# Causal scores of two heads in shared rows: an even head that needs 64 fewer keys per tile

## The reference

```python
q = (hidden_states @ Wq.T).reshape(bsz, q_len, N_HEADS, HEAD_DIM).transpose(0, 2, 1, 3)
q = q * cos + _rotate_half(q) * sin
k = jnp.repeat(k, GROUPS, axis=1)      # GROUPS = 4 query heads for each key head
v = jnp.repeat(v, GROUPS, axis=1)
scores = jnp.einsum('bhqd,bhkd->bhqk', q, k) * scale
scores = jnp.where(causal[None, None], scores, -1e9)
attn = jax.nn.softmax(scores, axis=-1)
out = jnp.einsum('bhqk,bhkd->bhqd', attn, v)
return out.transpose(0, 2, 1, 3).reshape(bsz, q_len, N_HEADS * HEAD_DIM) @ Wo.T
```

## Time and profile before

| what | value |
|---|---|
| median of 3 runs | 1459.31 us (1459.26 to 1460.89) |
| span of the profiled execution (first to last instruction) | 1457.5 us |
| granted clock of TensorE, mean | 1.000 |
| PE busy | 98% |
| DVE, POOL, ACT busy | 79%, 70%, 69% |
| DMA | 322.03 MB, 221 GB/s over the span |

### The profile page before, as it was taken

The page is one execution under the profiler, slowest core; times in us unless marked ns, Lnnn a source line. Parts: engine busy times, 40 slices in busy tenths (PEclk is TensorE's granted clock), DMA queues, the critical chain, the costliest instruction groups (busy, mean ns, idle before and its releaser), DMA issues.

```text
span 1457.5 us, 24651 instructions
## 1 busy us (share of the span) xinstructions
PE 1430.5 (98%) x7150; PEld 1208.2 (83%) x7150; DVE 1153.7 (79%) x3544; ACT 1006.8 (69%) x2389; POOL 1023.1 (70%) x805
## 2 busy tenths in 40 slices
PE   7989999999999999999999999999999999999998
PEld 7877888888888888888888888888888888888886
DVE  5697777777777777787777777777779998998876
ACT  5667666776776676767676677677677676776674
POOL 3767766876776677667676767677588888887662
PEclk9999999999999999999999999999999999999999
DMA  9478765875677667676677667758788899889872
GB/s 305 157 210 250 225 193 182 239 235 152 204 227 218 187 212 228 190 206 211 184 216 233 220 180 208 202 178 257 228 239 259 269 295 262 284 256 270 270 229 67
DMA packets 215157, 322.03 MB, mean 221 GB/s; under 512 B 42512, under 2 KB 132464, under 8 KB 215024
## 3 DMA queue, kind: packets, MB, share of 16 engines
q1 hardware_dynamic: 214736, 320.39, 73.7%
q10 hardware_dynamic: 288, 0.07, 0.0%
HBM read 179.43 MB, written 140.95 MB: 220 GB/s over the span
## 4 chain that ended last, share of the span: by engine, by line
PE 85%; POOL 4%; DVE 4%; DMA 2%; issue 2%; ACT 2%; SPq 0%; DVEq 0%; ACTq 0%
PE bank_s L634 22%; PE bank_o L794 21%; PE bank_pv L744 14%; PE bank_s L700 13%; PE bank_s L666 5%; PE bank_s L651 5%; POOL PT_lo L1836 2%; PE bank_s L696 1%; PE bank_s L607 1%; PE bank_s L850 1%; DVE y L1540 1%; DMA PT_raw<-blocks 1%; POOL qT_lo L1829 1%; DMA wc_scratch<-wc_out 1%; DVE blocks L1488 0%
## 5 line engine op out<-in xcount | busy, mean ns | idle before, releaser
L1836 POOL TENSOR_TENSOR PT_lo<-PT_raw,PT_hi 128x640 fp32r<-128x640 f32 x246 | 382.2, 1576 | 30.4 <-ACT PT_hi L1126 30.4
L1112 ACT ACTIVATE probs<-probs,row_inv 128x512 f32<-128x512 f32 (+3 forms) x512 | 257.8, 553 | 192.1 <-DVE row_inv L1471 192.1
L1824 POOL TENSOR_TENSOR rot_c<-rot_c,rot_s 128x512 f32<-128x512 f32 x128 | 167.7, 1310 | 257.7 <-DVE rot_s L1428 257.7
L1105 ACT ACTIVATE probs<-probs,row_min 128x384 f32<-128x384 f32 (+3 forms) x512 | 281.6, 552 | 49.2 <-DVE row_min L1464 49.2
L1488 DVE STREAM_TRANSPOSE blocks<-probs 128x384 f32<-128x384 f32 x508 | 213.7, 446 | 21.2 <-ACT probs L1112 13.0
L700 PE MATMUL bank_s<-kT_both,qT_hi 128*128 128x512 f32 (+2 forms) x768 | 215.2, 341 | 3.0 <-issue 1.3
L1464 DVE CUSTOM_DVE_ANT_0 probs<-bank_s,mask 128x512 f32<-128x512 f32 (+2 forms) x384 | 205.5, 552 | 0.8 <-issue 0.3
L1829 POOL TENSOR_TENSOR qT_lo<-rot_c,qT_hi 128x512 fp32r<-128x512 f32 x128 | 167.0, 1304 | 51.0 <-ACT qT_hi L1087 50.2
L634 PE MATMUL bank_s<-hT_lo,wq_hi 128*128 128x512 f32 x484 | 194.8, 403 | 2.2 <-DVE row_min L1464 1.4
L794 PE MATMUL bank_o<-wo_lo,OT_hi 128*128 128x512 f32 x496 | 195.1, 393 | 0.5 <-DVE rot_s L1428 0.5
L794 PE MATMUL bank_o<-wo_hi,OT_hi 128*128 128x512 f32 x496 | 193.4, 390 | 0.0
(11 more groups left out here) (315 smaller groups left out, 3255.0 us busy)
## 6 DMA issues: line engine op xcount, KB each, us to landing
blocks<-blocks SPq DMA_DIRECT2D x127, 640.0 KB, 3.5
PT_raw<-blocks SPq DMA_DIRECT2D x500, 160.0 KB, 3.9
stage<-in_wq SPq DMA_DIRECT2D x32, 256.0 KB, 5.1
vblocks<-kv_raw SPq DMA_DIRECT2D x32, 256.0 KB, 5.4
kv_raw<-vblocks SPq DMA_DIRECT2D x128, 64.0 KB, 2.3
stage<-in_wo SPq DMA_DIRECT2D x32, 256.0 KB, 5.1
split_wq<-wq_hi SPq DMA_DIRECT2D x32, 256.0 KB, 5.4
split_wq<-wq_lo SPq DMA_DIRECT2D x32, 256.0 KB, 5.7
```

The costliest lines, as they stand in the source:

```text
L1105: ins = act.activation(row(t, qt), row(t, qt), ACT.Exp, bias=row_min[m][:, qt:qt + 1], scale=-1.0, accum_out=row_sum[m][:, qt:qt + 1])
L1112: ins = act.activation(row(t, qt), row(t, qt), ACT.Copy, scale=row_inv[t % 2][:, qt:qt + 1])
L1824: pool.tensor_tensor(rot_c[:], rot_c[:], rot_s[:], ALU.add).then_inc(pool_a, 1)
L1836: pool.tensor_tensor(lo[:, at], raw_of(t)[:, at], hi[:, at].bitcast(F32), ALU.subtract).then_inc(pool_t, 1)
```

## The change

Heads 8 to 125 go in pairs that share their rows. Before, a row of a score tile was one of 128 queries of one head. Now the even step's tile holds the first 64 queries of that tile for both heads, interleaved (query, head, query, head), and the odd step's tile the last 64 of both. The rows of an even step therefore end 64 keys earlier, and its matmuls leave out those keys; the mask covers them in what follows. Both heads' queries must be there before either step's rows can be built: queries are projected four steps ahead instead of three (both t + 3 and t + 4 in step 6), the two rotated heads lie in one buffer, and each split takes half of the queries of both. The upper part of the odd step's queries is made in the even step before, ahead of the exponentials, and its lower part by DVE instead of POOL. Output products read their stationary operand with a step of two elements. A second mask (64 x 64 triangle, each row twice) is loaded before head 8, and the old one again before head 126. Reloads of wq for the fourth batch are issued one step earlier, and buffers that lay under the activations are waited for by the values projection (`pe_v`) instead of the query projection.

The core of the diff (further parts change names, buffers and the waits that go with them):

```diff
+HALF_TILE = P // 2
+MIXED_FROM, MIXED_TO = 8, ALL - 2
+BOTH_STEP = MIXED_FROM - 2
+EXTRA = MIXED_FROM + 2
+def two_heads(t):
+    return MIXED_FROM <= t < MIXED_TO
+def narrow(t):
+    return two_heads(t) and t % 2 == 0
+def projected(t):
+    ahead = [3] if t < BOTH_STEP else [3, 4] if t == BOTH_STEP else [4]
+    return [t + n for n in ahead if t + n < ALL]
+def low_by_pool(t):
+    return t < MIXED_FROM or t % 2 == 0
...
+        def in_row(w, t):
+            if two_heads(t):
+                return w.rearrange("p (q x h) -> p h q x", q=QT, h=2)
+            return w
+        def rotated(t):
+            if two_heads(t):
+                return rot_of(t)[:].rearrange("p h (q r x) -> p h q r x", r=2, x=HALF_TILE)[:, :, :, t % 2, :]
+            return rotated_head(t)
+        def head_rows(o, t, n):
+            if two_heads(t):
+                return o[:, 2 * n * P:2 * (n + 1) * P].rearrange("p (x h) -> p h x", h=2)[:, t % 2, :]
+            return o[:, (2 * n + t % 2) * P:(2 * n + t % 2 + 1) * P]
...
             def scores(t, tiles, before=None, now=None):
-                    pe.wait_ge(pool_q, t + 1)
+                    pe.wait_ge(pool_q, low_rows(t))
+                    if not low_by_pool(t):
+                        pe.wait_ge(dve_q, t + 1 - low_rows(t))
...
-                    keys = (qt + 1) * P
+                    keys = (qt + 1) * P - (HALF_TILE if narrow(t) else 0)
...
-                            mm = pe.matmul(bank[f"o{j}"][:], o[:, o_at:o_at + P], w[:, h, :],
+                            mm = pe.matmul(bank[f"o{j}"][:], head_rows(o[:], 2 * p + h % 2, j - tiles[0]), w[:, h, :],
...
             def step(t):            # PE
-                if 2 < t < ALL - 3:
-                    q_proj(t + 3)
+                for q in projected(t):
+                    q_proj(q)
...
             def q_split(t):         # ACT
-                act.wait_ge(pool_a, t + 1)
+                act.wait_ge(pool_a, t + 2 if t >= MIXED_FROM and t % 2 == 0 else t + 1)
                 if t >= 2:
                     act.wait_ge(pe_s, 4 * (t - 1))
-                act.activation(qT[t % 2][0][:], rot_c[:], ACT.Copy).then_inc(act_q, 1)
+                act.activation(in_row(qT[t % 2][0][:], t), rotated(t), ACT.Copy).then_inc(act_q, 1)
...
             def step(t):            # ACT
-                if h % 2 == 1 and t + 2 < ALL:
+                if h % 2 == 1 and t < BOTH_STEP:
                     q_split(t + 2)
...
                     split_moved_hi(t - 1)
+                if h % 2 == 0 and BOTH_STEP < t < ALL - 3:
+                    q_split(t + 3)
...
+            def q_split_lo(t):      # DVE
+                hi, lo = (in_row(w[:], t) for w in qT[t % 2])
+                dve.wait_ge(act_q, t + 1)
+                dve.tensor_tensor(lo, rotated(t), hi.bitcast(F32), ALU.subtract).then_inc(dve_q, 1)
...
                 invert_sums(t + 1, 0)
                 if h == 1:
                     v_split_lo(u)
-                if 2 < t < ALL - 3:
-                    q_rope(t + 3)
+                if h % 2 == 0 and BOTH_STEP < t < ALL - 3:
+                    q_split_lo(t + 3)
+                for q in projected(t):
+                    if q != EXTRA:
+                        q_rope(q)
...
             def step(t):            # POOL
-                    if t + 2 < ALL:
+                    if t < BOTH_STEP:
                         q_split(t + 2)
...
+            def load_mask(t):       # SP
+                sp.wait_ge(dve_s, QT * t)
```

More of the change, by code:

```diff
@@ L89, with query_step, low_rows, queries_read @@
 LATE_SPLITS = 6
+HALF_TILE = P // 2
[6 more added lines that the diff above has]
+    return two_heads(t) and t % 2 == 0
+def query_step(t):
+    return t - 3 if t < EXTRA else t - 4
+def projected(t):
[3 more added lines that the diff above has]
+    return t < MIXED_FROM or t % 2 == 0
+def low_rows(t):
+    return sum(low_by_pool(n) for n in range(t + 1))
+def queries_read(t):
+    return max([0] + [q + 1 for n in range(max(t - 1, 0)) for q in projected(n)])
 def q_offset(qt):
@@ L176, in build @@
         sin_t = whole.take("sin_t", [P, SEQ])
-        mask = whole.take("mask", [P, SEQ])
+        mask = whole.take("mask", [P, SEQ + HALF_TILE])
         y_at = whole.at
@@ L217, in build @@
         probs_end = whole.at
+        turned = Region(whole.at + 4 * SEQ).take("turned", [P, SEQ])
         qT = [[whole.take(f"qT_{p}{i}", [P, SEQ], F32R) for p in ("hi", "lo")] for i in range(2)]
@@ L234, in build @@
         small_end = whole.at
-        minus_half = whole.take("minus_half", [P, 1])
         assert whole.at <= nc.sbuf_usable_end
@@ L355, in q_bank, with rot_of, rotated_head, rotated_part @@
         def q_bank(t):
-            return bank["pv" if t < 5 else {5: "o3", 6: "o3"}.get(t, "s2" if third_first(t - 2) else "s3")]
+            if t < 7:
+                return bank["pv" if t < 5 else "o3"]
+            return bank["s2" if t == EXTRA or third_first(query_step(t) + 1) else "s3"]
+        def rot_of(t):
+            return extra_rot if t // 2 == EXTRA // 2 else rot
+        def rotated_head(t):
+            return rot_of(t)[:, t % 2 if t >= MIXED_FROM else 0, :]
+        def rotated_part(t):
+            if t >= MIXED_FROM and t % 2 == 1:
+                return turned[:]
+            return rot_of(t)[:, 1, :]
+        def in_row(w, t):
[10 more added lines that the diff above has]
+            return o[:, (2 * n + t % 2) * P:(2 * n + t % 2 + 1) * P]
         def logits_bank(t):
@@ L530, in again @@
             for u in range(AGAIN, UNITS):
[L531 removed]
+                found += [(f"wq{h}", u) for h in range(GROUP) if t == GROUP * u + h - 7]
                 found += [(f"wo{h}", u) for h in range(GROUP)
@@ L624, in q_proj @@
                     pe.wait_ge(dve_h, BATCH * CH)
-                elif t > 0:
+                elif t > 0 and t != EXTRA:
                     pe.wait_ge(dve_r, t)
                 if t > 6:
-                    pe.wait_ge(dve_s, score_read(t - 2, tile_order(t - 2)[0]))
+                    now = query_step(t) + 1 if t != EXTRA else BOTH_STEP + 1
+                    pe.wait_ge(dve_s, score_read(now, 2 if t == EXTRA else tile_order(now)[0]))
                 if t == GROUP * (SHARED - 1):
@@ L1451, in mask_and_max @@
                 m = t % 2
+                first = SEQ + HALF_TILE if narrow(t) else SEQ
                 if half == 0 and 0 < t <= BY_PE:
                     dve.wait_ge(dve_tp, t)
+                if half == 0 and t in (MIXED_FROM, MIXED_TO):
+                    dve.wait_ge(d_const, 80 if t == MIXED_FROM else 96)
                 for qt in half_order(t, half):
@@ L1458, in mask_and_max @@
                     if qt == 1:
-                        dve.tensor_tensor(row(t, 0), low_keys_bank, mask[:, SEQ - P:], ALU.add).then_inc(dve_low, 1)
+                        dve.tensor_tensor(row(t, 0), low_keys_bank, mask[:, first - P:first], ALU.add).then_inc(dve_low, 1)
                     if qt == 0:
@@ L1943, in step @@
                         k_split(u + 1)
-                    if t + 3 < ALL:
-                        q_rope(t + 3)
+                    for q in projected(t):
+                        q_rope(q)
+                        if t == BOTH_STEP and q != EXTRA:
+                            q_split(t + 2)
                     if t - FFN_FROM in EXPERT_STEPS:
```

92 lines of the change are left out of this document (56 added, 36 removed).

## The result

The changed kernel takes **1502.84 us** (median of 4 runs, 1498.58 to 1503.72), 1.0296 times the kernel before (95% interval 1.0282 to 1.0310; 1460.1 in the same session). The forecast was 1455.7. The profiled run has 1503.72 and a span of 1502.3, 44.8 more than before.

The account below looks back on a forecast made before the run. PE was taken as the bound (busy 98% of the span, 85% of the chain). Terms -11.7 + 6.6 + 1.5 = -3.6 on the span of 1457.5 gave 1453.9, plus 1.8 made 1455.7 us; range 1448 to 1469.

Parts of the forecast that it names:

- The size of the subtraction: DVE's new lower part of the odd head: 0.69 us of work plus waiting for POOL's running instruction, median over 0.8.
- Where its lateness goes: Even step: rope, transposes, block store and load come later; most pairs just covered, +1.5 us before 1060 us (0 to +18).
- Rival B: The blocks' store and load become the bound, PT_raw's load late in the odd step: +10.6, 1470 us; chance 0.26.
- Behind 1060 us: Router stretch: DVE's added subtraction against relief of y<-y,stage from POOL collisions, counted 0 us (bounds -2 and +5).
- A stretch behind 1060 us that changes by more than 5 us: Sign that the prediction is wrong, in the stretch where router work runs beside attention and 0 was counted.
- Part 1: Scores of 59 even heads: 64 fewer keys per query tile save 0.198 us per head, -11.7 us (-9.9 to -18.9).
- Part 2: Queries four steps ahead: wq3's lower part on POOL 0.95 us late in seven rounds, +6.6 us (4.5 to 12.6).
- tell-tale: Sign of being right: in steps 11, 23, ... 83 PE waits about 1 us for POOL's wq_lo.
- Strided operands: ACT, POOL and DVE writes and PE's wo weight loads with a step of two elements: taken as 0 us.
- Rival C: PE's weight loads with a step are four times slower, costing 300 us: about 1760 us; chance 0.04.
- The moved projection: One query projection moves from step 124 to step 6: counted 0 us, bounds -2.8 to +2.8.
- ACT's moved part: Odd head's upper part, 0.62 us, ahead of the even step's exponentials: hidden behind DVE's output additions or PE's projection.

Follow-up runs that it names:

- e7: Changed kernel with the second input of DVE's new subtraction read from PSUM instead of SBUF, size and place as before: 1477.28 us, ratio 1.0131.
- e6: Kernel before, with the score matmuls of even heads 8 to 124 leaving out 64 keys: 1455.30 us, ratio 0.9979.
- e10: Changed kernel with the second reciprocals ahead of DVE's new subtraction and wq3 split ahead of wv: 1490.15 us, ratio 1.0221.
- e3: Changed kernel with DVE's second reciprocals moved from behind the rope to ahead of the new subtraction in even steps: 1498.88 us, ratio 1.0278.
- e5: Kernel before, with the output products' stationary operand read with a step of two elements: 1466.22 us, ratio 1.0056.
- e14: As e13, with ACT's upper part of the odd row also cut from 512 to 8 columns: 1463.24 us, ratio 1.0039.
- e13: Changed kernel with DVE's subtraction reading one input from PSUM, wq3 split ahead of wv, output weights read without a step: 1463.00 us, ratio 1.0034.
- e2: Changed kernel with ACT's upper part of the odd row cut from 512 to 8 columns, semaphores kept: 1493.81 us, ratio 1.0249.
- e15: Changed kernel with even-step narrow scores, reciprocals first, wq3 before wv, earlier DVE subtraction, heads' rows side by side, block-row loads for 128 partitions: 2041.27 us.

## Why the prediction was wrong, by its steps

- **The size of the subtraction: right. Where its lateness goes: wrong, and this is the step that failed.** The text let the rope start 1.8 us later, and so it does. Then it followed the transposes, the store and the load of the blocks, and called the rest covered. The blocks were not late: PE waits 3.4 us in four places for PT_lo. Passed over were the second reciprocals, 0.17 us, that stand behind the rope on DVE; of the two, show only the first, ahead of it. On them hang ACT's scaling and chunk split, OT_hi, OT_lo and the one values bank. +1.5 was forecast for this up to 1060 us; PE waits 11.3 us for OT_lo before head 94. The wait for POOL is worth about 25 us over the whole run (e7). Rival B had the sign and the port, but the wrong loop.
- **Behind 1060 us: 0 forecast (bounds -2 and +5), +22.2 measured from head 94 to 124; the second half of the failed step.** The two sides of the sum were set equal without being added up. From head 94 to 124, the changed kernel's two lines and then the one of before:

```profile
L1518 DVE TENSOR_TENSOR qT_lo<-rot,qT_hi 128x512 fp32r<-128x512 f32 x15 | 23.9, 1594 | 0.0
...
L1633 DVE TENSOR_TENSOR y<-y,stage 128x512 f32<-128x512 f32 x12 | 9.9, 824 | 0.0
```

```profile
L1540 DVE TENSOR_TENSOR y<-y,stage 128x512 f32<-128x512 f32 x12 | 15.6, 1303 | 0.0
```

  The relief that the text named did come, but it is 5.7 us against 23.9, on an engine that was at 93% in part of this stretch. DVE's steps end late, and PE waits 12.0 us for `h` and 9.1 for OT_lo there. A stretch behind 1060 us that changes by more than 5 us was one of the text's own signs of being wrong.
- **Part 1: -11.7 forecast, -2.7 measured (e6).** The matmuls are as short as worked out: in the stalled pair's scores the 448-column ones start at 744.69 and 744.89, the 320-column ones at 745.44 and 745.59. The durations answer to the earlier trace rows:

```profile
L777 PE MATMUL bank_s<-kT_both,qT_hi 128*128 128x448 f32 x118 | 43.3, 367 | 1.9 <-issue 1.8
...
L777 PE MATMUL bank_s<-kT_both,qT_hi 128*128 128x320 f32 x118 | 35.5, 309 | 0.0
L777 PE MATMUL bank_s<-kT_both,qT_hi 128*128 128x192 f32 x118 | 28.1, 263 | 0.0
```

  The condition "as long as no other engine's result becomes late" was not checked at the place where the columns go: the earlier trace rows show the values product right behind the scores, and what else it waits for was not asked.
- **Part 2: +6.6 forecast, 8.7 measured (e10 against e3)**; 7.2 in the seven steps that were named, 5.6 of it as a wait for wq_lo. The mechanism and the size were right. But its tell-tale was bad: in the changed kernel PE is held in the same steps by OT_lo first, and the row shows 0.9 in one place.
- **Strided operands: 0 forecast, +8.2 measured (e5).** By the Trainium skill, "SBUF — State Buffer", section "Door 1: The DMA port swizzle", a step of two fp32 should have been free; for PE's weights the measurement says 6 to 8 ns each. Rival C's 300 us is far off. ACT's split with the step takes 662 ns at the median, 622 before.
- **The moved projection: 0 forecast, bounds 2.8.** Step 6 takes 2.2 more, and only 0.6 comes back at the end.
- **ACT's moved part: hidden**, as forecast, once the other causes are gone (e14 against e13). Beside the waiting subtraction it isn't: without it the changed kernel is 9.0 us faster (e2), all of it behind head 94.

Taken away one after the other, the wait gives 25.6 us (e7), order and step of two together 14.3 more (e13), and 4.8 over before stay. The single prices, -2.7 + 8.7 + 8.2 + 25.6 + 2.2 - 0.6 = 41.4, come near the 44.8 of the spans too, but they were measured in different kernels and overlap, so that nearness shows nothing.

## What to carry to other kernels

Where work is taken away, ask at that place what the next instruction waits for besides its own engine: the gain ends at the longest of these waits. Where an instruction is put into a queue, list all that stands behind it, the shortest too, and follow each to who waits for it. Where an instruction waits for one that runs on a neighbour engine, as DVE with two SBUF inputs does here for POOL, its price is what is left of the neighbour's and not its own size: place it where the neighbour changes over, or read one input from elsewhere (0.69 us from PSUM). And where two changes of load on a nearly full engine seem to cancel, add both up from their rows.

## What was new about the hardware

- DVE with two SBUF inputs waits for the POOL instruction that runs, whatever its own size: 1.1 us at the median for 8 columns and 1.64 for 512 at the same place, 0.69 flat with one input in PSUM. By the moment it is asked for, the same instruction took 0.69 to 0.99 or 1.73 to 2.11 (changed kernel, heads 12 to 90). The Trainium skill, "SBUF — State Buffer", section "Who interferes with whom", states this for a DVE instruction with two SBUF inputs and a GpSimd one that reads SBUF, and the traces agree.
- PE's weights with a step of two elements: output products 0.234 instead of 0.226 us apart.
- One DMA for 128 partitions was slower than one for 32. The pages count packets, changed kernel and e15:

```profile
DMA packets 215445, 322.20 MB, mean 214 GB/s; under 512 B 42544, under 2 KB 132752, under 8 KB 215312
```

```profile
DMA packets 209782, 322.19 MB, mean 158 GB/s; under 512 B 36880, under 2 KB 127088, under 8 KB 209648
```

  The bytes are the same, and 5664 small packets are missing: 12 for each of the 472 loads that changed form. The Trainium skill, "DMA: Bandwidth & Descriptors", section "Rules for kernel authors", says that an outermost dimension of fewer than 16 confines a DMA to at most as many engines; the new form has 4 outermost (block columns), the old 32. Sixteen less four is the 12 that is missing, which fits; no trace here names the DMA engines, and a form for 128 partitions with more outermost was not tried, so this cause is argued and not shown.
